# GpSimd makes every fourth source one-hot of the eight-chunk counting loop

## The reference, cut to what matters

```python
out_deg = segment_sum(ones, src)               # and in_deg by dst
agg = segment_sum((h * norm_src)[src], dst)    # layer 0; the others have the same form
x = layernorm(x + elu(agg * norm_dst @ W + b))
```

## Time and profile before

| | us |
|---|---|
| median of 3 runs | 1914.79 |
| lowest, highest | 1913.35, 1915.44 |
| the profiled execution | 1920.13 |
| its span, from the first to the last instruction | 1918.4 |

### The profile page before, as it was taken

How to read it: one execution, slowest core, us unless ns; L and a number is a source line. 1 busy time by engine, 2 the same in 40 slices (tenths; PEclk the granted TensorE clock), 3 DMA queues, 4 the chain that set the end, 5 groups by cost and what they waited for, 6 DMA issues and landing times.

```text
span 1918.4 us, 35049 instructions
## 1 busy us (share of the span) xinstructions
PE 1755.1 (91%) x9445; PEld 1414.5 (74%) x9479; DVE 957.2 (50%) x2851; ACT 482.1 (25%) x1262; POOL 494.4 (26%) x899
## 2 busy tenths in 40 slices
PE   3999996999988999999999999999999699999971
PEld 2456665788878888788878877877777489899851
DVE  7877774444455411122211127767777544444466
ACT  0044554322223211122221111112212123222323
POOL 1022223211123200000000002217888843223214
PEclk7999997999999999999999999999999799999986
DMA  5068889999779888877768889997777499999981
GB/s 136 35 282 336 360 362 377 327 323 324 271 274 361 322 291 290 255 215 215 210 199 302 287 258 291 290 276 247 259 262 242 131 328 371 371 371 372 373 303 67
DMA packets 339452, 535.59 MB, mean 279 GB/s; under 512 B 17871, under 2 KB 275322, under 8 KB 332442
## 3 DMA queue, kind: packets, MB, share of 16 engines
q1 hardware_dynamic: 329514, 516.24, 80.2%
q0 software_dynamic: 7888, 17.23, 2.4%
q10 hardware_dynamic: 1952, 0.95, 0.3%
HBM read 405.95 MB, written 128.41 MB: 279 GB/s over the span
## 4 chain that ended last, share of the span: by engine, by line
PE 60%; SPq 11%; DMA 8%; issue 7%; POOL 6%; DVE 5%; DVEq 2%; ACT 1%; ACTq 0%; POOLq 0%
PE psum L1128 41%; PE psum L1225 4%; DMA blk<-counts_src_on_rows 4%; PE psum L1018 4%; PE psum L1015 3%; SPq L494 3%; SPq L508 2%; PE psum L600 2%; POOL expert_rows_in L1998 2%; POOL pick_and_gate_of_row L2015 2%; PE psum L1037 2%; SPq L500 2%; PE psum L612 1%; SPq L497 1%; SPq L504 1%
## 5 line engine op out<-in xcount | busy, mean ns | idle before, releaser
L1128 PE MATMUL psum<-xsa,blk 128*128 128x512 f32 x2500 | 640.0, 403 | 5.5 <-DVE xsa L1694 2.8
L1128 PEld LDWEIGHTS psum<-xsa,blk 128*128 128x128 f32 x2500 | 455.8, 189 | 95.7 <-issue 6.1
L1128 PE MATMUL psum<-xsb,blk 128*128 128x512 f32 (+1 forms) x1875 | 406.9, 366 | 14.4 <-DMA blk<-counts_src_on_rows 10.2
L1128 PEld LDWEIGHTS psum<-xsb,blk 128*128 128x128 f32 x1875 | 314.8, 189 | 68.9 <-issue 14.1
L1976 POOL TENSOR_SCALAR ve<-mv 128x1 f32<-128x1 f32 x75 | 16.8, 223 | 760.7 <-DVE mv L1670 760.7
L1555 DVE TENSOR_SCALAR onehots<-counts_scratch 128x348 bf16<-128x348 f16 x464 | 162.6, 377 | 64.1 <-issue 40.1
L600 PE MATMUL psum<-route,expert_weights 128*128 128x128 f32 x1296 | 166.1, 282 | 2.4 <-DVE route L712 2.0
L1015 PE MATMUL psum<-onehots 128*128 128x349 bf16 x464 | 148.4, 320 | 19.1 <-DVE onehots L1560 17.1
L1018 PE MATMUL psum<-zrow 128*128 128x512 bf16 x431 | 163.3, 387 | 0.0
L600 PEld LDWEIGHTS psum<-route,expert_weights 128*128 128x128 f32 x1296 | 154.3, 195 | 11.5 <-DVE route L712 2.7
L612 PE MATMUL psum<-expert_weights,route 128*128 128x256 f32 x648 | 153.4, 380 | 0.2 <-ACT route L666 0.2
(11 more groups left out here) (317 smaller groups left out, 2114.6 us busy)
## 6 DMA issues: line engine op xcount, KB each, us to landing
blk<-counts_src_on_rows SPq DMA_DIRECT2D x125, 832.0 KB, 6.0
blk<-counts_src_on_rows SPq DMA_DIRECT2D x125, 768.0 KB
expert_weights<-in_L_gnn_w SPq DMA_DIRECT2D x162, 512.0 KB
blk<-counts_dst_on_rows SPq DMA_DIRECT2D x50, 832.0 KB, 5.5
counts_dst_on_rows<-band_rows SPq DMA_DIRECT2D x25, 1600.0 KB, 5.6
blk<-counts_dst_on_rows SPq DMA_DIRECT2D x50, 768.0 KB
counts_src_on_rows<-blk SPq DMA_DIRECT2D x13, 1600.0 KB, 8.9
counts_src_on_rows<-rblk SPq DMA_DIRECT2D x12, 1600.0 KB, 9.5
```

What stands on the lines that cost most here:

```text
L1128: mm = e.matmul(o, blk[n][:, k * P:(k + 1) * P], XS[:, k, :, 0:Fw], start=(k == 0), stop=(k == T - 1 and not own), skip_group_check=True)
```

## The change

In the loop by eight, the fourth and the eighth source one-hot are made by GpSimd, into two more slots (4 and 5) that only it writes. VectorE skips these two and makes the other six and all target one-hots; in the loop by four it makes all as before. GpSimd first copies the chunk's two keys (`scol` and `wcol`, which now lie side by side) to a small buffer at a fixed address, waits for that copy, waits until TensorE is done with the slot's last use (one chunk more than that, in fact), and then runs the same TENSOR_SCALAR as VectorE. TensorE waits for those two on a semaphore of their own, `lent_ready`. GpSimd's pipeline over the bands is now unrolled, with the stages `lent_sources` of band b, `cast` of band b - 1 and `none_lent` of band b, which walks the loop by four to keep its two semaphores in step and reads the bounds of the next band. Of the 464 source one-hots, 86 go to GpSimd.

```diff
--- before.py
+++ after.py
@@ -201,7 +201,7 @@
             return region.enter_context(nc.sbuf_tensor(name, shape, dt, align_bytes=64))
 
         xsb = rg("counts_scratch", [P, 20480], BF16)
-        xsa = rg("onehots", [P, UNROLL * (FW + 2 + P)], BF16)
+        xsa = rg("onehots", [P, (UNROLL + 2) * (FW + 2) + UNROLL * P], BF16)
 
         digits = rg("digits", [P, BYTES, FW], I32)
         wide_s = rg("wide_onehots", [P, FIELDS * FW], BF16)
@@ -224,7 +224,11 @@
         bandcol, at = view(xsb, at, 8, F32)
         bandrow, at = view(xsb, at, 5 * 32, F32)
         dcol, at = view(xsb, at, EG * P, F32)
-        scol, at = view(xsb, at, EG * P, F32)
+        v, at = view(xsb, at, 2 * EG * P, F32)
+        source_keys = v.rearrange("p (c two) -> p c two", two=2)
+        scol, wcol = [source_keys[:, :, k] for k in range(2)]
+        v, at = view(xsb, at, 2 * 2, F32)
+        lent_keys = v.rearrange("p (n two) -> p n two", two=2)
         fcol, at = view(xsb, at, EG * P, F32)
         srccol, at = view(xsb, at, EG * P, F32)
         icol, at = view(xsb, at, EG * P, I32)
@@ -237,13 +241,12 @@
             words[n], at = view(xsb, at, FW + 2, I32)
         assert at <= 20480
 
-        wcol = src_rows
         one_w = FW + 2
-        one_s, at = view(xsa, 0, UNROLL * one_w, BF16)
-        one_s = one_s.rearrange("p (b s) -> p b s", b=UNROLL)
+        one_s, at = view(xsa, 0, (UNROLL + 2) * one_w, BF16)
+        one_s = one_s.rearrange("p (b s) -> p b s", b=UNROLL + 2)
         one_d, at = view(xsa, at, UNROLL * P, BF16)
         one_d = one_d.rearrange("p (b s) -> p b s", b=UNROLL)
-        assert at <= UNROLL * (FW + 2 + P)
+        assert at <= (UNROLL + 2) * (FW + 2) + UNROLL * P
 
         region.close()
         XSa = rg("xsa", [P, T, PARTS, F], F32R)
@@ -381,6 +384,14 @@
             middle = e.snap(e.to_reg(start + (more >> 1) * (2 * UNROLL)), min_val=0, max_val=1 << 15)
             upto = e.snap(e.to_reg(start + more * UNROLL + UNROLL), min_val=0, max_val=1 << 15)
             return e.snap(e.to_reg((v & 511) - start), min_val=-(1 << 15), max_val=511), start, middle, upto
+
+        def lent_slot(n, by):
+
+            return UNROLL + n // UNROLL if by > UNROLL and n % UNROLL == UNROLL - 1 else None
+
+        def chunk_index(k, own, n):
+            return nc.s_assert_within(k + own + n, 0, EC + 3 * UNROLL,
+                                      skip_runtime_bounds_check_because="k runs from the band's start to its end")
 
         def next_groups(e, b, start):
 
@@ -1011,8 +1022,9 @@
                             u = n % UNROLL
                             if u % PAIR == 0:
                                 e.wait_ge(S("targets_ready"), k + n + PAIR)
-                            e.wait_ge(S("sources_ready"), k + n + 1)
-                            e.matmul(o, one_d[:, u, :], one_s[:, u, 0:FW + 1], start=False, stop=True,
+                            lent = lent_slot(n, by)
+                            e.wait_ge(S("sources_ready" if lent is None else "lent_ready"), k + n + 1)
+                            e.matmul(o, one_d[:, u, :], one_s[:, u if lent is None else lent, 0:FW + 1], start=False, stop=True,
                                      skip_group_check=True).then_inc(S("onehots_used"), 1)
 
                             e.matmul(psum[:, par, 0:BANK], zrow[:, 0:P], zrow[:, 0:BANK], start=False, stop=True,
@@ -1540,20 +1552,20 @@
             def chunk_loop(b, many, ends, lo, hi, by):
                 own = ends[0]
                 with e.Fori(ends[lo], ends[hi], by) as k:
-                    def chunk(n):
-                        return nc.s_assert_within(k + own + n, 0, EC + 3 * UNROLL,
-                                                  skip_runtime_bounds_check_because="k runs from the band's start to its end")
-                    many(b, k, chunk, by)
+                    many(b, k, lambda n: chunk_index(k, own, n), by)
 
             lanes = [P, PAIR, P // 2, 2]
 
             def packed(b, k, chunk, by):
                 for n in range(by):
-                    c, u = chunk(n), n % UNROLL
+                    u = n % UNROLL
+                    if lent_slot(n, by) is not None:
+                        continue
+                    c = chunk(n)
 
                     e.wait_ge(S("onehots_used"), k + n + 1)
                     e.tensor_scalar(one_s[:, u, 0:FW], iota_f, scol[:, bass.ds(c, 1)], wcol[:, bass.ds(c, 1)],
-                                    ALU.is_equal, ALU.mult).then_inc(S("sources_ready"), 1)
+                                    ALU.is_equal, ALU.mult).then_inc(S("sources_ready"), 1 if lent_slot(n + 1, by) is None else 2)
                     if u % PAIR == 0:
 
                         e.wait_ge(S("onehots_used"), k + n + PAIR)
@@ -1949,7 +1961,34 @@
                     e.wait_ge(S("digits_cut"), len(MASKS) * b + m + 1)
                     carry_wait(e)
                     e.tensor_copy(fields_of(band_rows[par], m), digit(m)).then_inc(S("lower_cast"), 1)
-            pipeline(e, [(1, cast), (3, nothing)])
+            ends_of = [groups_of(e, 0), None]
+
+            def lent_sources(b, par):
+                own, before, middle, _ = ends_of[par]
+                with e.Fori(before, middle, 2 * UNROLL) as k:
+                    for n in range(UNROLL - 1, 2 * UNROLL, UNROLL):
+                        c, turn = chunk_index(k, own, n), n // UNROLL
+                        keys = lent_keys[:, turn, :]
+                        e.tensor_copy(keys, source_keys[:, bass.ds(c, 1), :].rearrange("p c two -> p (c two)"))\
+                            .then_inc(S("keys_taken"), UNROLL)
+
+                        e.wait_ge(S("keys_taken"), k + n + 1)
+                        carry_wait(e)
+                        e.wait_ge(S("onehots_used"), k + n - 2)
+                        carry_wait(e)
+                        e.tensor_scalar(one_s[:, lent_slot(n, 2 * UNROLL), 0:FW], iota_f, keys[:, 0:1], keys[:, 1:2],
+                                        ALU.is_equal, ALU.mult).then_inc(S("lent_ready"), UNROLL)
+
+            def none_lent(b, par):
+                _, _, middle, upto = ends_of[par]
+                e.wait_ge(S("lent_ready"), middle)
+                carry_wait(e)
+                with e.Fori(middle, upto, UNROLL) as k:
+                    e.sem_inc(S("keys_taken"), UNROLL)
+                    e.sem_inc(S("lent_ready"), UNROLL)
+                if b + 1 < T:
+                    ends_of[1 - par] = next_groups(e, b + 1, upto)
+            pipeline(e, [(0, lent_sources), (1, cast), (0, none_lent), (3, nothing)], unrolled=True)
 
             e.wait_ge(S("degrees_read"), 1)
             for g in range(T // SPLIT):
```

## The result

The changed kernel takes 1934.28 us (median of 4, 1932.86 to 1936.94) against 1914.07 us for the kernel before in the same rounds: a ratio of 1.0102, 95% interval [1.0089, 1.0115]. Of 1914.8 us that is 19.5 us more. The forecast was 7.8 us more: the right side, and the measured time is inside the range, but the loss is two and a half times the one forecast.

The account below looks back on a forecast made before the run. VectorE was taken to bound long bands and set the length of short ones; 0.415 us held against 0.28 saved loses 0.135 in 58 groups, 7.8 us on 1914.8, giving 1922.5 us, range 1908 to 1939.

Parts of the forecast that it names:

- by 0.11 us a group: Long bands of counting: VectorE's 1.565 us for four chunks exceeds TensorE's floor of 1.45 by 0.11.
- I take 0.60 us: Duration assumed for GpSimd's lent one-hot, a little above the 0.51 us from ops reading one tensor.
- the bound of 0.96 above it: Upper estimate for GpSimd's one-hot, from an op reading two tensors at 2.1 ns an element: 0.96 us.
- rival 2: GpSimd's one-hot is slow, toward 0.96 us: 58 x 0.50 = 29 us lost, 1943 us; chance 0.15.
- what would show it wrong: In counting: VectorE's turn of eight at TensorE's 2.9 us, or TensorE's waits ending at GpSimd.
- Its turn of eight was 3.40 us: VectorE's turn of eight chunks in the first band, forecast at 3.40 us.
- The sum by the page's figure: With the Trainium skill's 2.03 cycles an element, GpSimd's one-hot takes some 0.81 us; loss some 20 us instead of 8.
- a lent one-hot stops VectorE for about its own duration less 0.185: In counting, GpSimd's op holds VectorE for all but a 0.185 us handover: 0.415 us with a 0.60 us op.
- the term was 0.415: Time each lent one-hot holds VectorE in counting, 0.415 us, set against 0.28 us saved.
- the wider strides of the keys at setup are two short ops: Side-by-side keys at setup: two short ops in front of a wait for the loads, costing nothing.
- 58 groups x 0.135: Of 86 lent one-hots in counting, 58 pay 0.135 us each: 7.8 us lost.

Follow-up runs that it names:

- one_more_step: The kernel before, with one semaphore step that nobody waits for ahead of each of VectorE's 464 source one-hots: ratio 1.0116, 22.2 us above.
- eighth_last_apart: The change with GpSimd making only the eighth one-hot of each turn (43) and VectorE's keys in separate buffers: ratio 1.0005, 1.0 us above the kernel before.
- keys_alone: The kernel before with only the keys laid side by side, nothing lent to GpSimd: ratio 1.0088, 16.9 us above.
- lent_apart: The whole change, but VectorE reads its keys from two buffers as before: ratio 1.0087, 16.7 us above the kernel before.
- forms_alone: The kernel before, with GpSimd's op forms timed behind all its work; whole time not compared, counting bands one and 24 end at 70.67 and 296.75 us.
- none_made: The change with GpSimd's key copies and one-hots removed, its queue and waits kept, VectorE making all 464: ratio 1.0070, 13.4 us above the kernel before.
- eighth_unused_apart: The change with GpSimd making 43 one-hots nobody uses, VectorE making all 464 with keys in separate buffers: ratio 1.0041, 7.9 us above the kernel before.

## Why the prediction was wrong

**Right:** that VectorE is the bound in the long bands of the kernel before, by 0.11 us a group (one_more_step, which slows VectorE's queue alone, slows the kernel); that the two engines disturb each other in this loop; that the loss lies in counting (the last band ends 18.0 us later, and the span is 16.4 us longer); the sign, though not for its reason.

**Wrong, "I take 0.60 us", and the bound of 0.96 above it.** This is the step that failed first. The op takes 1.63 us. Both bounds came from how many tensors an op reads. By the forms alone what counts is the arithmetic: a copy 0.48, one operation 1.15, two operations 1.55 us for 348 elements. The largest term missed follows from it: the forecast gave GpSimd's own cycle a price of nothing, and rival 2 said that it "stays under VectorE's 1.28 + 0.78". That holds for 0.96 us, where the cycle would be some 1.5, and not for 1.63, where it is 2.14 and the bound. The forecast named what would show it wrong, and that is what came: TensorE's waits end at GpSimd (11.6 us). Its turn of eight was 3.40 us and is 4.28.

The Trainium skill, GPSIMD Engine Reference, section 7, has 2.03 cycles an element for a compare-and-select; with the 3.4 ns measured, at that page's 1.2 GHz (section 1), this op takes some 4.1, an estimate from that clock. The sum by the page's figure came to 20 us and the measured loss is 19.5, but by chance: neither its duration nor its mechanism was the one that acts.

**Wrong, "a lent one-hot stops VectorE for about its own duration less 0.185".** That held for a cast, 0.87 of 1.055 us. For the one-hot it would give 1.4 us, and measured are 0.21 (long bands) and 0.2 to 0.3 (short). The forecast's own sum with the measured 1.63 us would have been 58 x 1.165 = 68 us, so its two wrong terms pulled opposite ways. The cast takes 1.0 ns an element and the one-hot 4.7. That VectorE is held by the reading and writing of elements and not by the computing on them is my reading of this; no run shows it. By the size alone the term was 0.415 for 0.21 to 0.3: too high, and against 0.28 saved it leaves next to nothing, as eighth_last_apart has it (1.0 us).

**Missed, "the wider strides of the keys at setup are two short ops".** I costed the layout where it is written and not where it is read: at every source one-hot in VectorE's queue, one register instruction more each. That is worth 16.9 us by itself (keys_alone), and 2.8 on top of GpSimd's cycle (19.5 against lent_apart's 16.7). What the queue held was in the profile to be asked for: line 1555 has one register instruction of 93 ns per op.

**The sum itself, 58 groups x 0.135**, has the right sign for the wrong reason, and that is luck: its 0.135 was a held time too long less a saved time. Of the loss, the first band has 8.9 us, which is GpSimd's cycle (lent_apart has 8.4 of it, keys_alone 3.3), and the rest up to the 24th band 8.7, where keys_alone has 7.4 and lent_apart 6.4. Against forms_alone in place of the kernel before, the first band has 10.2 us and the rest 10.1. They overlap, so no exact split exists.

## What to carry to other kernels

When work moves to GpSimd, price its whole cycle: the op by its count of operations per element, the helper copy, and the waits between them. Compare that with the pace of the loop before looking at anything else. When a buffer's layout changes for one engine, count what the other engines' queues now do to address it, at every use; where ops of 0.3 us follow one another, one more register or semaphore instruction per op is on the path. And before tuning a division of labour, run it with the lent work left out: none_made showed in one run that the frame of the change can cost two thirds of the loss with no work on GpSimd.

## What the runs showed of the hardware that I had not expected

- A two-operation TENSOR_SCALAR on GpSimd costs 3.4 ns more for each element (1.53 to 1.56 us for 348 with VectorE idle), one operation takes 1.15 us, a copy 0.48 us (forms_alone).
- One semaphore step per source op in VectorE's queue took a turn of eight from 3.13 to 3.92 us, 0.1 us for each of its eight source ops, though each op is busy for 0.37 as before (one_more_step).
- GpSimd's one-hot held VectorE for 0.2 to 0.3 us in all (eighth_unused_apart, forms_alone), its cast of 1.05 us for 0.87. VectorE held the one-hot as well: 2.07 us in a turn of the first band of eighth_unused_apart, against 1.53 to 1.56 alone.
